# Moving a small subtraction from GpSimd to VectorE in a graph attention kernel, and closing the first group with one tile

## What is computed

```python
h = jnp.maximum(_layernorm(x, axis=-1), 0.0)
# _L0_gnn_ref(h, adj, W, a1, a2):
h = x @ W.T
src = h @ a1
dst = h @ a2
e = leaky_relu(src[:, None] + dst[None, :], negative_slope=0.2)
e = jnp.where(adj == 0, -9e15, e)
h_prime = softmax(e, axis=1) @ h
x = x + h_prime
```

## Time and profile before

| what | value |
| --- | --- |
| median of 3 runs | 406.71 us (406.16 to 409.22) |
| span of the profiled execution | 404.4 us |
| TensorE busy in it | 390.9 us (97%) |
| VectorE busy in it | 371.7 us (92%) |
| ScalarE busy in it | 201.9 us (50%) |
| GpSimd busy in it | 69.0 us (17%), 44.0 us of it in the 32 subtractions of L337 |

### The profile page before, as it was taken

The page is one execution under the profiler, slowest core; times in us unless marked ns, Lnnn a source line. Parts: engine busy times, 40 slices in busy tenths (PEclk is TensorE's granted clock), DMA queues, the critical chain, the costliest instruction groups (busy, mean ns, idle before and its releaser), DMA issues.

```text
span 404.4 us, 9752 instructions
## 1 busy us (share of the span) xinstructions
PE 390.9 (97%) x3396; PEld 333.5 (82%) x3396; DVE 371.7 (92%) x457; ACT 201.9 (50%) x291; POOL 69.0 (17%) x73
## 2 busy tenths in 40 slices
PE   7999999899999799999999999999999999999995
PEld 7787678787878588888888888888888888888884
DVE  2999698999999989999998799999998799999965
ACT  3799864545455453444444624445444435544430
POOL 1423055354545212000000021000000120000000
PEclk9999999999999899999999999999999999999998
DMA  7920068555555567766666657666665576666503
GB/s 230 370 78 2 3 208 316 201 195 186 186 192 185 161 204 229 229 217 224 220 220 218 195 167 224 223 220 216 216 222 174 181 225 218 220 220 218 186 0 107
DMA packets 26261, 77.90 MB, mean 193 GB/s; under 512 B 3296, under 2 KB 8960, under 8 KB 26112
## 3 DMA queue, kind: packets, MB, share of 16 engines
q1 hardware_dynamic: 25088, 74.48, 56.6%
q0 software_dynamic: 1152, 3.15, 2.2%
HBM read 73.40 MB, written 4.21 MB: 192 GB/s over the span
## 4 chain that ended last, share of the span: by engine, by line
PE 68%; DVE 21%; DMA 4%; issue 3%; ACT 1%; SPq 1%; DVEq 0%; ACTq 0%
PE ps L819 64%; DVE p_lo L622 9%; DVE p_sb L615 7%; DMA adj_sb<-adj_t 2%; DMA c_flat<-c_turned 1%; DVE stats L495 1%; DMA x_sb<-x 1%; PE ps L781 1%; DVE rows_sb L682 1%; PE ps L766 1%; PE ps L777 1%; PE ps L778 1%; DVE hnt_lo L511 1%; DVE hn_sb L518 1%; ACT hnt_hi L392 0%
## 5 line engine op out<-in xcount | busy, mean ns | idle before, releaser
L819 PE MATMUL ps<-v_sb,p_hi 128*128 (+2 forms) x2048 | 255.0, 273 | 4.0 <-DVE p_lo L622 3.0
L425 ACT ACTIVATE p_hi<-p_sb,p_scale 128x1024 f16<-128x1024 f32 x127 | 145.7, 1149 | 172.1 <-DVE p_sb L615 148.3
L819 PEld LDWEIGHTS ps<-v_sb,p_hi 128*128 128x128 f16 x2048 | 199.0, 97 | 32.8 <-issue 4.4
L622 DVE SCALAR_TENSOR_TENSOR p_lo<-p_sb,p_scale,p_hi 128x1024 f16<-128x1024 f32 x128 | 175.3, 1370 | 9.6 <-ACT p_hi L425 9.6
L615 DVE SCALAR_TENSOR_TENSOR p_sb<-c_row,g_col,adj_sb 128x1024 f32<-128x1024 uint32 (+1 forms) x127 | 162.6, 1282 | 1.6 <-DMA adj_sb<-adj_t 1.6
L819 PE MATMUL ps<-v_sb,p_lo 128*128 (+1 forms) x1024 | 143.5, 274 | 2.1 <-DVE p_lo L622 2.1
L819 PEld LDWEIGHTS ps<-v_sb,p_lo 128*128 128x128 f16 x1024 | 97.7, 98 | 22.2 <-DVE p_lo L622 9.7
L337 POOL TENSOR_TENSOR v_sb<-h_sb,v_sb x32 | 44.0, 1374 | 52.9 <-ACT v_sb L403 52.7
L344 POOL DMA_DIRECT2D out<-rows_sb x24 | 13.2, 551 | 182.0 <-DVE rows_sb L639 180.6
L495 DVE BATCH_NORM_STATS2 stats<-x_sb 128x6 f32<-128x256 f32 x32 | 12.7, 405 | 7.1 <-DMA x_sb<-x 7.1
L331 POOL TENSOR_SCALAR hn_sb<-x_sb,moments,rstd 128x256 f32<-128x256 f32 x8 | 10.7, 1339 | 26.7 <-DVE shift L506 26.7
(11 more groups left out here) (89 smaller groups left out, 114.0 us busy)
## 6 DMA issues: line engine op xcount, KB each, us to landing
adj_sb<-adj_t SPq DMA_DIRECT2D x128, 512.0 KB, 4.8
x_sb<-x SPq DMA_DIRECT2D x8, 512.0 KB, 8.0
out<-rows_sb POOLq DMA_DIRECT2D x24, 128.0 KB, 2.7
c_row<-c_flat SPq DMA_DIRECT2D x1, 1536.0 KB, 6.8
out<-rows_sb SPq DMA_DIRECT2D x8, 128.0 KB, 1.8
w_nat<-w SPq DMA_DIRECT2D x1, 256.0 KB, 2.5
w_f<-w_t SPq DMA_DIRECT2D x1, 256.0 KB, 3.0
a_sb<-a SPq DMA_DIRECT2D x2, 1.0 KB, 2.5
```

Source lines behind the costliest of these rows:

```text
L425: nc.scalar.activation(p_hi[:, u % R, :], p_sb[:, u % R, :], ACT.Copy, scale=p_scale[:, bass.ds(t, 1)])\
L622: nc.vector.scalar_tensor_tensor(out=p_lo[:, u % R, :], in0=p_sb[:, u % R, :], scalar=p_scale[:, bass.ds(t, 1)], in1=p_hi[:, u % R, :], op ...
L819: return nc.tensor.matmul(ps[:, k, 0:width], part[:, u % R, k * P:(k + 1) * P], v_sb[:, bass.ds(t, 1), v, 0:width], start=start, stop=stop ...
```

## The change

The low parts of the values leave GpSimd: its loop over 32 tiles is deleted. VectorE makes them with the same operation, for tile t between `p_sb` of tile t and `p_lo` of tile t - 1; that of tile 0 comes between the first and second piece of `p_sb` of tile 0. ScalarE makes the high parts one tile ahead: that of tile t + 1 before its `p_hi` of tile t. For the first group only, the closing sums cover one tile instead of two, so tile 30 is done as the others are. The other groups keep two.

```diff
-            with pool.Fori(0, T) as t:
-                pool.wait_ge(v_hi_ready, t + 1)
-                nc.gpsimd.tensor_tensor(v_sb[:, bass.ds(t, 1), 1, 0:F], h_sb[:, bass.ds(t, 1), 0:F],
-                                        v_sb[:, bass.ds(t, 1), 0, 0:F], ALU.subtract).then_inc(v_lo_ready, 1)
...
-            def tiles_group0(q, first):
+            def tiles_group0(q, first, last):
                 for u in range(U):
-                    t = q * U + u
+                    if not (last and u == U - 1):
+                        values_hi(q * U + (u + 1))
                     if first and u == 0:
                         split_first_parts()
                     else:
-                        values_hi(t)
-                        split_hi(u, t, q * U)
-            tiles_group0(0, True)
-            with act.Fori(1, Q) as q:
-                tiles_group0(q, False)
+                        split_hi(u, q * U + u, q * U)
+            tiles_group0(0, True, False)
+            with act.Fori(1, Q - 1) as q:
+                tiles_group0(q, False, False)
+            tiles_group0(Q - 1, False, True)
...
+            def values_lo(t, n):
+                dve.wait_ge(v_hi_ready, n)
+                nc.vector.tensor_tensor(v_sb[:, bass.ds(t, 1), 1, 0:F], h_sb[:, bass.ds(t, 1), 0:F],
+                                        v_sb[:, bass.ds(t, 1), 0, 0:F], ALU.subtract).then_inc(v_lo_ready, 1)
...
+                if m == 0:
+                    values_lo(0, 1)
...
                         edge_weights(u, q * U + u, q * 32 + 16 * (u // R + 1), 0)
-                    if u > 0 or not first:
+                        values_lo(q * U + u, q * U + (u + 1))
                         split_lo(u - 1, q * U + (u - 1), q * U)
...
-            def last_sums(t, n):
+            def last_sums(t, n, closing):
...
-                    for u in (U - 2, U - 1):
+                    for u in range(U - closing, U):
...
+                closing = 1 if g is None else 2
+                for u in range(U - closing if last else U):
```

More of the change, by code:

```diff
@@ L853, in last_sums @@
                         done = product(u, t + u, k, p_lo, 0, False, u == U - 1)
-                        if u == U - 2 and k == RB - 1:
+                        if u < U - 1 and k == RB - 1:
                             done.then_inc(slot_free, 1)
@@ L859, in tiles @@
                 n = q * U if g is None else g * T + q * U
-                for u in range(U - 2 if last else U):
+                closing = 1 if g is None else 2
+                for u in range(U - closing if last else U):
                     if g is None:
@@ L866, in tiles @@
                         pe.wait_ge(v_lo_ready, T)
-                    last_sums(q * U, n)
+                    last_sums(q * U, n, closing)
             def group(g):
```

## The result

The changed kernel takes 403.66 us (median of 8 runs, 403.32 to 404.45) against 406.40 (8 runs, 405.82 to 409.30): a ratio of 0.993, with a 95% interval of 0.991 to 0.996. Timed again beside the last group of experiments it took 403.98 us against 406.37, 0.994 (0.992 to 0.996). The gain is 2.7 and 2.4 us. The forecast was 403.8, a gain of 2.95 on the 406.71 of the kernel before's first three runs.

A forecast was written before the change was run, and what follows sets the result against it. TensorE bounds it from 138.56 us, VectorE's pace the first group. VectorE arrives 0.83 us earlier, the closing puts TensorE 3.7 ahead, VectorE's later row caps that at 2.95: 406.71 - 2.95 = 403.8 us, range 402.7 to 406.0.

The forecast's parts named there:

- X: Time from the start of VectorE's new low-part operation to the next operation's start; forecast 0.34 us.
- Rival 2: The new VectorE operation gives its neighbour no overlap, 0.424 us between starts; gain 0.7, 406.0 us; chance 6%.
- rival 4: New wait and addresses stall VectorE 0.13 us ahead of each new operation; slower, 407.3 us; chance 5%.
- Rival 1: The new operation takes 0.395 us between starts, as with a scalar from memory; gain 1.5, 405.2 us; chance 18%.
- Rival 7: New operation below 0.30 us between starts, or unseen slack in VectorE's row to tile 6; gain above 4; chance 8%.
- rival 5: GpSimd isn't what lengthens first-group p_lo, so 26 tiles keep their 0.39 us; 10.1 us lost, 413.9; chance 3%.
- Start: First group's opening tiles: p_sb(3) comes 0.22 us later, and through the load of tile 8 p_sb(8) goes to 70.79.
- Closing: First group's end: TensorE idles 0.3 us, not 3.00, does 24 products, and is 3.7 us ahead after 16 second-group products.
- rival 3: TensorE's clock falls at the group's turn all the same; gain 2.0, 404.7 us; chance 7%.
- Rival 6: The closing saves nothing, as TensorE waits for ScalarE's copies as long as it had worked; gain 0.8, 405.9; chance 6%.
- The cap: VectorE's row of work from second-group tile 2 to 6 lets TensorE get at most 2.95 us ahead.
- second term: At the first group's closing, TensorE's clock stays at 1.00 instead of falling for 3.6 us at 0.53.

The follow-up runs named there:

- e3: Changed kernel with the new VectorE operation multiplying by a scalar of one read from memory; 405.22 us, ratio 0.997.
- e5: Changed kernel with GpSimd also doing its subtraction, into a spare buffer nobody reads; 414.58 us, ratio 1.019.
- e6: Changed kernel with GpSimd writing a constant into 1024 spare columns once a tile, reading nothing; 403.81 us, ratio 0.992.
- e1: Kernel before with only the one-tile closing of the first group, low parts still on GpSimd; 404.60 us, ratio 0.996.
- e8: Changed kernel with VectorE's output rows spread one a tile over 8 tiles, not two a tile over 4; 403.60 us, ratio 0.992.
- e2: Changed kernel with the old two-tile closing, so only the low parts moved; 405.39 us, ratio 0.998.
- e12: The changed kernel itself, timed again beside the last group of experiments; 403.98 us, ratio 0.994.

## Why the prediction was right

All times here are counted from the first `p_sb` (47.96 before, 48.51 after), to leave out what the load of `x` did. The mechanism came out as forecast, term by term. That the time came within 0.14 us of the forecast is partly luck: the kernel before was 0.3 lower over eight runs than over the three that the sum started from, and the gain was 0.2 smaller.

- **X.** Forecast 0.34 with a length of 424 ns; measured 0.33 (94.26 to 94.59) and 413. Rival 2 (0.424, no overlap) falls with it, and rival 4 (the new waits and addresses cost 0.13): the new operation starts 1.20 after the `p_sb` ahead of it. The flush between operations that the Trainium skill describes ("VectorE: DVE Perf Modes", "Terms") does not show as a gap between recorded operations: the next start comes 80 ns before the recorded end. The formula of the Trainium skill (same page, section on the TRN2 errata) gave 327 ns and meets the distance between starts of the new operation, but not its 413 ns of length, nor the 1195 ns between starts of the large one. Rival 1 was a true price for another instruction: e3 measured it at 0.40. Rival 7 falls too, with X above 0.30.
- **Pace.** 71.24 to 133.97 over 23 tiles is 2.727 a tile, forecast 2.73. e5 and e6 together show the cause that the forecast only read from rows: rival 5 falls.
- **Start.** Tile 7's load, behind which SP's store stands, waits for `p_sb` of tile 3: a load waits for the `p_sb` of four tiles before it, not three. p_sb(1) came 0.33 later and p_sb(3) 0.21 (forecast 0.34 and 0.22), p_sb(8) 0.12 instead of 0.22: the load behind `c_row` took 0.1 less after its release. VectorE reached the second group 0.99 earlier (137.89 against 138.33), forecast 0.83; the load and the pace make up the difference.
- **Closing.** 24 products, 0.23 us of idle time, granted clock 1.00: rival 3 falls. Eight copies take 2.29, (2.29 - 0.39) / 7 = 0.27 each, forecast 0.265. The first 16 products of the second group were done at 144.03, 3.8 ahead (forecast 3.7). Rival 6 falls, and e1 shows the closing's share by itself.
- **The cap.** p_lo of second-group tile 2 came at 145.17, 2.6 ahead (2.45), and TensorE's waits stand at tiles 5 and 6, where they were put. The last wait ended 3.1 ahead (160.62 against 163.18), forecast 2.95; the excess is the 0.16 of VectorE's arrival. e8 removed this cap and the waits with it.

What the prediction mis-sized is the constancy of its second term. It took the low clock of the earlier trace rows as part of the kernel before, 1.65 us in each execution. e2 shows it absent after the same wait. In such an execution of the kernel before, the second group would start that much earlier, and the change would win some 1.4 us instead of 3.05 (an estimate: 3.05 less the 1.65 that e2 lacks).

How often it comes can be bounded. Each run beside the experiments has the mean granted clock of its execution on record. Of the 61 runs of the kernel before, 10 have 1.000, so they hold no low stretch of that size anywhere, and their median is 404.8 us; the other 51 have 406.8. The changed kernel has three such runs of 18, with a median of 403.0, against 403.9 for the rest. So at most 51 of 61 executions of the kernel before had the low clock at the closing. It may be fewer, since a mean below 1.00 can come from elsewhere, as in e1 (0.59 from 8 to 16 us) and e2 (0.63 at 76 to 80 us). The sum of the halves, 3.1 against 2.4 to 2.7, is within the intervals and settles nothing.

One slip in the prediction changes nothing here: its tails of 9% and 4% are a point each above the rivals that they name, 8% and 3%.

## What to carry to other kernels

Before an operation is moved from GpSimd, ask what its reads cost VectorE: here 0.4 us of VectorE for each subtraction, more than the 0.33 for which VectorE does the work itself. Price a small operation by the distance between starts and by its exact form, since it is paid once per tile on the engine that sets the pace. When a stage is shortened, find what is late next (ScalarE's copies, then VectorE's row of work), and look for the transfer that a large one holds up: loading ahead of it and splitting it was worth as much as the whole change. And ask of every term read from one trace whether it is there in every execution: here a clock that fell in some of them was 1.65 us of a gain of 3.05.

## What the runs showed of the hardware

- A scalar read from memory costs VectorE 0.06 us per operation on 128 x 256 elements (476 against 413 ns, 0.40 against 0.33 between starts).
- GpSimd subtractions of 128 x 256 and two-input VectorE operations shut each other out, 0.38 to 0.48 us of VectorE each; GpSimd writes of 128 x 1024 without a read cost nothing (e5, e6).
- TensorE's granted clock fell to its lower level after idle times of 3.00 us (before), 2.58 (e12), 2.54 (e8) and 2.38 (e2, at tile 8). It stayed at 1.00 after 2.96 (e2, at the closing), 2.44 (e6) and 2.43 (e3). In these runs the idle time alone does not tell whether the clock falls.
- The same low level cost 1.65 us where TensorE was the engine that others waited for (the closing, before), some 1.26 at the start of e12, and nothing behind tile 8, where VectorE sets the pace (e2, e8, e12).
- The load behind the 1.5 MB broadcast kept VectorE waiting 1.5 to 1.8 us in some executions and 2.4 to 2.6 in others of the same order of work. With tile 8's load ahead of the broadcast, and that in three pieces, the wait was gone, and the runs lay closer together (within 0.8 us over six, against 3.5 over ten).
